# Two reorderings in a one-core audio block: ScalarE's copies of chunks 1 and 2 against a square root and a table load, and the readers of the identity against a memset

## Chip, cores and metric

The kernel runs on one core of a Trainium2 chip. The metric is the device time of one execution in microseconds (us); lower is better. A core has five engines with their own instruction streams: TensorE (PE), VectorE (DVE), ScalarE (ACT), GpSimd (POOL) and SyncE (SP, here a DMA queue). They meet only at semaphores: an instruction that has done its work increments one, and an engine waits until one has reached a value. Each engine issues in program order, so a wait holds up all that is queued behind it.

## The reference

```python
# x: (4, 32, 750); h: (4, 750, 128)
def tok(x):                       # token layer
    x_diff = first difference over time (first row 0)
    x_emb = x_diff @ W_ve.T + b_ve
    x_smooth = (ewma(x_emb) + flip(ewma(flip(x_emb)))) * 0.5     # alpha 0.1
    return x_smooth @ W_lin.T + b_lin
def attn(x):                      # 4 heads of 32
    q, k = l2norm(x @ q_w), l2norm(x @ k_w)
    v = x @ (basis @ v_coeffs.T)
    scores = (q @ k.T) * decay ** (distance - 1) * (key later than query)
    return (scores @ v) @ (basis @ o_coeffs.T).T * out_scale
def ffn(x):                       # over the 128 features
    return gelu(x @ tril(W1).T + b1) @ tril(W2).T + b2
h = tok(x)
h = h + attn(layernorm(h))
h = h + ffn(layernorm(h))
```

## The kernel before, in words

The smoothing is linear, so the kernel smooths the 32 input channels of 4 batches (128 partitions, 750 steps) to `z` and multiplies by combined weights afterwards. Time is cut into 6 chunks of 125 steps. Attention looks only forward in time, so the chunks are taken from the end: step i of the program handles chunk 5 - i, and a `state` of 32x32 per head and batch is carried on. The order on every engine is written out by hand.

**Setup.** GpSimd builds the identity (lines 263 and 265), the shifted mask `before` (267, 269), `minus_half` (271), and then writes 180.0 (`ONE`) into two rows of `z_stk` (line 274; 2 partitions x 3000 elements). It signals these with `ident_ok`, `before_ok`, `half_ok` and `zone_ok`. Behind them it waits for the feed-forward weights and cuts both to triangles (line 278), which waits for `zone_ok` too. VectorE starts with memsets: `keep` (536, 537), `keep_b` (538 to 540), `first_one`, `ones_blk` and `floor_c` (541 to 549). Then it waits for the identity and reads it twice: `centre` is the identity less 1/128 (line 551, `centre_ok`), `pick` repeats parts of it (line 552, 128x384, `pick_ok`). Behind those it works on the input: a difference (`xd`, 564), a backward scan (`bwd`, 561), a partial sum (569), two halves of the forward scan (`fwd`, 583 and 587) and `z` (575) for the last chunk, then the backward scan, difference, sum and `z` for the one before it. SyncE's queue brings the tail of `x` first, then its first half, then weights; ScalarE's queue brings the rest of `x` and `w_tok`.

**First product.** TensorE's `select` (line 838) moves `z` of a chunk into the layout of `z_stk`; it waits for `pick_ok` and `z0_ok` and stands in TensorE's order behind the product of line 825. ScalarE writes its high words (389), VectorE its low words (604), and `project_qk(0)` (917, 920) reads them, with `zone_ok` as another condition. GpSimd computes `z` of the four earlier chunks (286, 289, 292) in three passes with two inputs each; VectorE's backward scan over 500 steps (line 561) feeds the last.

**Norms.** The squared norms come in two groups: group 0 covers steps 0 and 1, group 1 steps 2 to 5. `sums` on VectorE writes them, `turn_sums` on TensorE turns them (897), `roots` on ScalarE takes the square root (456, `root_ok`), `scales` on VectorE makes the reciprocals (641, 645, 647).

**ScalarE around the change.** `roots(1)` is followed by a dummy Gelu (line 501), ahead of which the compiler puts the load of the Gelu table. Then come `q_out(2)`, `k_out(2)` (403, 410), `r_out(1)` (423) and `h_out(1)` (416), which copy PSUM banks to SBUF. TensorE's `attention_out(1)` (1026) waits for the last two. Then TensorE runs `scores(2)` (971), which waits for `root_ok`, and `ffn_turn(0)` (1047), which waits for `xn` of `normed(0)` on ScalarE (433). `normed(0)` needs `rstd` from GpSimd's `rsqrt(0)` (326, 330), which stands behind `add_b2(0)` (340) and `distance(2)` (318, needs `qT` of `q_out(2)`). The loop for steps 2 to 4 follows.

Of the kernel before, what the change touches and what calls it, by code (L numbers as in the profile page):

```python
# [7 lines left out]
ALU = mybir.AluOpType  # L8
ACT = mybir.ActivationFunctionType

B, CH, T = 4, 32, 750
D = 128
# [21 lines left out]
def build(nc, x, w_tok, w_att, w_base, w_ffn, out):  # L34
    with ExitStack() as ctx:
        def sb(name, shape, dt=F32):
            return ctx.enter_context(nc.sbuf_tensor(name, shape, dt))

        def sem(name):
            return ctx.enter_context(nc.semaphore(name))  # L40
# [3 lines left out]
        ident, centre = IC[:, 0, :], IC[:, 1, :]  # L44
        pick = sb("pick", [D, B, 3 * CH])
# [36 lines left out]
        table_in = sb("table_in", [D, 1])  # L82
# [6 lines left out]
        keep = sb("keep", [D, T])  # L89
# [17 lines left out]
        def bufs(name, shape):  # L107
# [28 lines left out]
            for n in ("s0_ps", "s1_ps", "s2_ps", "s3_ps", "r_ps", "a_ps"))  # L136
# [9 lines left out]
        pool_c, ident_ok, centre_ok, tril_ok, ones_ok, half_ok, before_ok, zone_ok, one_ok, zero_ok, floor_ok = (  # L146
            sem(n) for n in ("pool_c", "ident_ok", "centre_ok", "tril_ok", "ones_ok",
                             "half_ok", "before_ok", "zone_ok", "one_ok", "zero_ok", "floor_ok"))

        table_ok, exp_ok, dec_u, dec_ok, pow_ok, dmask_ok, keypow_ps, keypow_ok = (  # L150
            sem(n) for n in ("table_ok", "exp_ok", "dec_u", "dec_ok", "pow_ok", "dmask_ok", "keypow_ps",
                             "keypow_ok"))
# [10 lines left out]
        zstk_d, pick_ok, sel_s, selhi_ok, sello_ok = (  # L163
            sem(n) for n in ("zstk_d", "pick_ok", "sel_s", "selhi_ok", "sello_ok"))
# [18 lines left out]
        def flat(tile):  # L183
            return tile.rearrange("p b f -> p (b f)")

        def batches(part):
            return (0, B) if part is None else (part * B // 2, (part + 1) * B // 2)
# [5 lines left out]
        def turned_sums(group):  # L193
            return r_ps[0:C, 2 * D:2 * D + 2 * GR] if group == 0 else s0_ps[0:C, 0:4 * GR]
# [3 lines left out]
        def h_bank(i):  # L198
            return k1_ps if i == LAST else a_ps
# [62 lines left out]
        def _(pool):  # L262
# [8 lines left out]
            pool.memset(minus_half[:, :], -0.5).then_inc(half_ok, 1)  # L271
            pool.wait_ge(before_ok, 1)
            pool.wait_ge(half_ok, 1)
            pool.memset(z_stk[3 * CH:STK, :, :, :].bitcast(F32), ONE).then_inc(zone_ok, 1)
            pool.wait_ge(ffn_in_d, 16)
            pool.wait_ge(zone_ok, 1)
# [81 lines left out]
        def _(act):  # L358
# [39 lines left out]
            def q_out(i):  # L398
                act.wait_ge(q_s, i + 1)
                if i >= NBUF:  # L400
                    act.wait_ge(qd_ok, i - NBUF)
                    act.wait_ge(score_s, H * (i - NBUF + 1))
                act.activation(flat(qT[i % NBUF][:, :, :]), s2_ps[:, 0:W4], ACT.Copy).then_inc(qT_ok, 1)  # L403
# [8 lines left out]
            def h_out(i):  # L412
                act.wait_ge(h_s, i + 1)
                if i >= NBUF:
                    act.wait_ge(h2_ok, B * (i - NBUF + 1))
                act.activation(flat(h_tok[i % NBUF][:, :, :]), h_bank(i)[0:C, :], ACT.Copy, scale=1.0 / ONE).then_inc(h_ok, 1)  # L416

            def r_out(i, part=None):
                b0, b1 = batches(part)
                act.wait_ge(rT_s, i + 1)  # L420
                if i >= NBUF:
                    act.wait_ge(at_s, i - NBUF + 1)
                act.activation(flat(rT[i % NBUF][:, b0:b1, :]), r_ps[:, b0 * C:b1 * C], ACT.Copy).then_inc(rT_ok, 1)  # L423

            def normed(i):

                n = i % NBUF
                act.wait_ge(rstd2_ok, i + 1)
                act.wait_ge(h2_ok, B * (i + 1))
                if i >= NBUF:  # L430
                    act.wait_ge(xT_s, i - NBUF + 1)
                for b in range(B):
                    act.activation(xn[n][:, b, :], h2[n][:, b, :], ACT.Copy, scale=rstd2[n][:, b:b + 1])\  # L433
                        .then_inc(xn_ok, 1)

            def ffn_in(i, part=None):
                n, (b0, b1) = i % NBUF, batches(part)
                act.wait_ge(xT_s, done(i, part))
                if i >= NBUF:
                    act.wait_ge(f1_s, i - NBUF + 1)  # L440
                act.activation(flat(xT[n][:, b0:b1, :]), turn_bank(i, part)[:, b0 * C:b1 * C], ACT.Copy)\
                    .then_inc(xT_ok, 1)
# [9 lines left out]
            def roots(group):  # L452

                c0, c1 = GROUPS[group]
                act.wait_ge(sst_ps, group + 1)
                act.activation(nrm[:, :, c0 * B:c1 * B].rearrange("p a (c b) -> p a c b", b=B),
                               turned_sums(group).rearrange("p (c a x) -> p a c x", a=3, x=CH)[:, :, :, 0:B],
                               ACT.Sqrt).then_inc(root_ok, 1)
# [38 lines left out]
            gram_out(5)  # L497
            h_out(0)
            r_out(0)
            roots(1)  # L500
            act.activation(table_in[:, :], keep[:, 0:1], ACT.Gelu).then_inc(table_ok, 1)  # L501
            q_out(2)
            k_out(2)
            r_out(1)
            h_out(1)
            for i in range(2, LAST):
                normed(i - 2)
                ffn_in(i - 2)
                h_out(i)
                ffn_gelu(i - 2)  # L510
                q_out(i + 1)
                k_out(i + 1)
                r_out(i)
# [21 lines left out]
        def _(dve):  # L535
            dve.memset(keep[:, 0:1], 10.0 * (1.0 - ALPHA)).then_inc(keep_ok, 1)
            dve.memset(keep[:, 1:T], 1.0 - ALPHA).then_inc(keep_ok, 1)
            dve.memset(keep_b[:, 0:1], ALPHA - 1.0).then_inc(keep_ok, 1)
            dve.memset(keep_b[:, 1:2], 9.0 / ALPHA).then_inc(keep_ok, 1)
            dve.memset(keep_b[:, 2:C + 1], 1.0 - ALPHA).then_inc(keep_ok, 1)  # L540
# [4 lines left out]
            for b in range(B):  # L545
# [1 line left out]
                dve.memset(ones_blk[b * CH:(b + 1) * CH, 1, b:b + 1], 1.0).then_inc(ones_ok, 1)  # L547
            dve.memset(floor_c[0:2 * CH, :], 0.0).then_inc(floor_ok, 1)
            dve.memset(floor_c[2 * CH:GR, :], EPS_LN * ONE * ONE).then_inc(floor_ok, 1)
            dve.wait_ge(ident_ok, 1)  # L550
            dve.tensor_scalar(centre, ident, -1.0 / D, None, ALU.add).then_inc(centre_ok, 1)  # L551
            dve.tensor_copy(pick[:, :, :].rearrange("p b (a c) -> p b a c", a=3),
                            ident.rearrange("p (b c) -> p b c", b=B).unsqueeze(2).broadcast_to([D, B, 3, CH]))\
                .then_inc(pick_ok, 1)

# [78 lines left out]
            def scales(group):  # L636

                k, cols = 2 * group, slice(GROUPS[group][0] * B, GROUPS[group][1] * B)
                n = cols.stop - cols.start
                dve.wait_ge(root_ok, group + 1)  # L640
                dve.scalar_tensor_tensor(out=nrm[:, 0:2, cols], in0=nrm[:, 2:3, cols].broadcast_to([C, 2, n]),
                                         scalar=EPS_L2, in1=nrm[:, 0:2, cols], op0=ALU.mult, op1=ALU.max)\
                    .then_inc(stat_v, 1)
                dve.wait_ge(stat_v, k + 1)
                dve.reciprocal(rec[:, :, cols], nrm[:, :, cols]).then_inc(stat_v, 1)
                dve.wait_ge(stat_v, k + 2)
                dve.tensor_tensor(sc_v[:, cols], rec[:, 1, cols], rec[:, 2, cols], ALU.mult).then_inc(scale_ok, 1)
# [39 lines left out]
            def carry_on(i):  # L687

                dve.wait_ge(st_s, i + 1)
                new = flat(state[i % NBUF][:, :, :])  # L690
                if i == 0:
                    dve.tensor_copy(new, st_ps).then_inc(st_ok, 1)
                else:
                    if i >= NBUF:
                        dve.wait_ge(rT_s, i - NBUF + 2)
                    dve.wait_ge(st_ok, i)
                    dve.wait_ge(pow_ok, 1)
                    dve.scalar_tensor_tensor(out=new, in0=flat(state[(i - 1) % NBUF][:, :, :]), scalar=chunk_pow,
                                             in1=st_ps, op0=ALU.mult, op1=ALU.add).then_inc(st_ok, 1)
# [27 lines left out]
            def statistics(i, part=None):  # L727

                n, (b0, b1) = i % NBUF, batches(part)
                for b in range(b0, b1):  # L730
                    dve.wait_ge(h2_ok, B * i + b + 1)
                    dve.bn_stats(bn6[n][:, b, :], h2[n][:, b, :]).then_inc(bn_ok, 1)  # L732
                if i >= NBUF:
                    dve.wait_ge(ve2_ok, i - NBUF + 1)
                for b in range(b0, b1):
                    dve.wait_ge(bn_ok, B * i + b + 1)
                    dve.bn_aggr(mv[n][:, b, :], bn6[n][:, b, :]).then_inc(mv_ok, 1)
# [34 lines left out]
            residual(0)  # L772
            keys(1)
            statistics(0)
            scales(1)
            carry_on(1)

            for i in range(2, LAST):
                residual(i - 1)
# [411 lines left out]
```

## Time and profile before

| what | value |
|---|---|
| median of 3 runs | 84.05 us (84.0 to 87.06) |
| profiled execution, its own time | 83.98 us |
| span in its profile | 82.3 us |
| PE busy | 68.0 us (83%) |
| DVE busy | 60.6 us (74%) |
| ACT busy | 40.9 us (50%) |
| POOL busy | 37.4 us (45%) |

The span runs from the first to the last event of the engines that the profiler saw; 1.68 us of the execution's own time lie outside it. Busy times of different engines overlap. In a row of the timeline, the numbers in front are start and duration in us, "xN" the instructions merged in the row, and the bracket the idle time of that engine just before the row with the event that ended it. In the chain, each row is a piece of the sequence that ended last, with the time that it contributes.

### The profile page before, as it was taken

Reading aid. Unit: us, or ns where it says so; the run is one execution under the profiler, and the core shown is the slowest. Engines: PE = TensorE matmul, PEld = TensorE weight load, DVE = VectorE, ACT = ScalarE, POOL = GpSimd, SP = SyncE. Lnnn points to the kernel's source line nnn. Section 1 sums busy time; section 2 is a strip of 40 time slices with the busy share of each in tenths; the row PEclk is TensorE's granted clock in tenths of the full one; section 3 lists DMA queues with packets and bytes.
Section 4 is the critical chain, followed back from the end, with each engine's and each line's share of the span. In section 5 each row is a group of like instructions: output and inputs, shape, how many; then the busy total and the mean of one; then the engine's idle time right before and its main releaser. Section 6 shows DMA issues by size and latency. Waiting matters only on the chain.

```text
span 82.3 us, 2682 instructions
## 1 busy us (share of the span) xinstructions
PE 68.0 (83%) x1047; PEld 51.4 (63%) x1047; DVE 60.6 (74%) x177; ACT 40.9 (50%) x94; POOL 37.4 (45%) x48
## 2 busy tenths in 40 slices
PE   2996759964975899855999999999999997978840
PEld 2984648641143784645967996798679975845730
DVE  5799999999056493994998599848993599694250
ACT  1536345679365200494765366626663624574420
POOL 5935194396563700278423833292409100667800
PEclk9999999999999999999999999999999999999997
DMA  0960000001433100000000040003000300003043
GB/s 8 288 228 0 0 0 0 8 0 52 104 97 93 39 0 0 8 0 0 0 8 4 0 132 1 0 8 125 4 0 8 115 14 8 0 0 125 0 137 113
DMA packets 3826, 3.55 MB, mean 43 GB/s; under 512 B 2171, under 2 KB 3189, under 8 KB 3814
## 3 DMA queue, kind: packets, MB, share of 16 engines
q1 hardware_dynamic: 3474, 3.06, 12.9%
q10 hardware_dynamic: 340, 0.32, 1.2%
q8 instruction: 8, 0.13, 0.7%
q14 instruction: 4, 0.03, 0.1%
HBM read 1.08 MB, written 1.54 MB: 32 GB/s over the span
## 4 chain that ended last, share of the span: by engine, by line
PE 61%; DVE 20%; ACT 7%; issue 7%; POOL 1%; DVEq 0%; ACTq 0%; POOLq 0%
PE s_ps L971 8%; PE s_ps L1059 6%; PE a_ps L1026 6%; PE r_ps L1000 6%; PE s_ps L1076 5%; PE r_ps L986 5%; PE s_ps L875 4%; PE k_ps L929 3%; DVE prob L658 3%; PE s_ps L917 3%; DVE ident_and_centring L551 2%; PE r_ps L1047 2%; PE a_ps L951 2%; DVE ss_row L633 2%; ACT L501 2%
## 5 line engine op out<-in xcount | busy, mean ns | idle before, releaser
L658 DVE TENSOR_TENSOR prob<-s_ps,dmask 125x500 f32<-125x500 f32 x24 | 15.0, 673 | 1.7 <-PE s_ps L971 1.5
L340 POOL TENSOR_TENSOR h_b<-h,w_ffn 125x512 f32<-125x512 f32 (+1 forms) x7 | 7.8, 1133 | 11.4 <-DVE h L722 9.2
L318 POOL TENSOR_TENSOR q_dec<-qT,powers 128x500 f32<-128x500 f32 x5 | 5.8, 1163 | 9.8 <-ACT qT L403 9.8
L433 ACT ACTIVATE xn<-h,rstd 125x128 f32<-125x128 f32 x20 | 6.4, 390 | 5.8 <-POOL rstd L330 5.8
L301 POOL TENSOR_TENSOR quad<-gram_z,z 128x250 f32<-128x250 f32 (+1 forms) x6 | 5.9, 997 | 5.0 <-ACT gram_z L467 3.7
L722 DVE SCALAR_TENSOR_TENSOR h<-a_ps,rec,h_tok 125x128 f32<-125x128 f32 x22 | 6.2, 343 | 2.2 <-PE a_ps L1026 2.2
L971 PE MATMUL s_ps<-qT,kT 32*125 32x125 f32 x192 | 6.9, 279 | 0.9 <-ACT gram_z L467 0.9
L708 DVE TENSOR_TENSOR y<-s_ps,h_b 125x512 f32<-125x512 f32 (+1 forms) x6 | 3.9, 647 | 4.8 <-PE s_ps L1076 4.8
L971 PEld LDWEIGHTS s_ps<-qT,kT 32*125 32x125 f32 x192 | 5.9, 183 | 2.4 <-issue 2.1
L1026 PE MATMUL a_ps<-o_T,rT 128*125 128x128 f32 x44 | 5.9, 274 | 1.9 <-ACT h_tok L416 1.9
L330 POOL TENSOR_TENSOR rstd<-ve,minus_half 125x4 f32<-125x4 f32 (+1 forms) x7 | 6.6, 944 | 0.6
L1026 PEld LDWEIGHTS a_ps<-o_T,rT 128*125 128x125 f32 x44 | 5.3, 187 | 2.4 <-ACT rT L423 2.2
L1000 PE MATMUL r_ps<-prob,v_sc 125*32 125x125 f32 x192 | 6.4, 272 | 0.5 <-DVE prob L658 0.5
L1076 PE MATMUL s_ps<-w_ffn,gT 128*125 128x128 f32 x44 | 6.2, 283 | 0.2 <-ACT gT L449 0.2
L1000 PEld LDWEIGHTS r_ps<-prob,v_sc 125*32 125x32 f32 x192 | 4.9, 109 | 2.0 <-issue 1.8
L1059 PE MATMUL s_ps<-xT,w_T 128*128 128x500 f32 (+1 forms) x12 | 5.9, 576 | 0.0
L1076 PEld LDWEIGHTS s_ps<-w_ffn,gT 128*125 128x125 f32 x44 | 5.3, 187 | 0.9 <-issue 0.6
L986 PEld LDWEIGHTS r_ps<-q_dec,state 32*32 32x32 f32 x160 | 4.0, 104 | 2.4 <-issue 2.2
L449 ACT ACTIVATE gT<-s_ps,w_att 128x500 f32<-128x500 f32 (+1 forms) x6 | 3.9, 642 | 3.1 <-PE s_ps L1059 3.1
L986 PE MATMUL r_ps<-q_dec,state 32*32 32x125 f32 x160 | 5.3, 268 | 0.0
L423 ACT ACTIVATE rT<-r_ps 128x500 f32<-128x500 f32 (+1 forms) x7 | 3.6, 527 | 3.5 <-PE r_ps L1000 3.5
L732 DVE BATCH_NORM_STATS2 bn<-h 125x6 f32<-125x128 f32 x24 | 5.3, 278 | 0.0
(175 smaller groups left out, 147.2 us busy)
## 6 DMA issues: line engine op xcount, KB each, us to landing
out_dram<-y SPq DMA_DIRECT2D x5, 224.0 KB
z_stk<-z_hi SPq DMA_DIRECT2D x8, 62.5 KB, 2.1
z_stk<-z_lo SPq DMA_DIRECT2D x4, 62.5 KB, 2.1
out_dram<-y SPq DMA_DIRECT2D x2, 112.0 KB
w_base<-in_w_base_dram SPq DMA_DIRECT2D x1, 192.0 KB, 3.6
w_ffn<-in_w_ffn_dram SPq DMA_DIRECT2D x1, 192.0 KB, 3.6
xt<-in_x_dram SPq DMA_DIRECT2D x1, 188.0 KB, 3.0
w_tok<-in_w_tok_dram ACTq DMA_DIRECT2D x1, 162.0 KB, 3.2
```

The costliest lines, as they stand in the source:

```text
L301: pool.tensor_tensor(quad[:, a, t0:t1], gram_z[piece % 2][:, 0:t1 - t0], z[:, t0:t1], ALU.mult)\
L330: pool.tensor_tensor(rstd2[n][:, b0:b1], ve2[n][:, b0:b1], minus_half[:, b0:b1], ALU.pow)\
L340: pool.tensor_tensor(h2_b[n][:, b0:b1, :], h2[n][:, b0:b1, :], b2_row.unsqueeze(1).broadcast_to([C, b1 - b0, D]), ALU.add)\
L433: act.activation(xn[n][:, b, :], h2[n][:, b, :], ACT.Copy, scale=rstd2[n][:, b:b + 1])\
L658: dve.tensor_tensor(prob[i % 2][:, h, :, :], sc_ps[h][0:C, 0:W4].rearrange("p (b t) -> p b t", b=B), dmask[:, h, :].unsqueeze(1).broadcast ...
L722: dve.scalar_tensor_tensor(out=h2[n][:, b, :], in0=att_bank(part)[0:C, b * D:(b + 1) * D], scalar=rec[:, 0, at:at + 1], in1=h_tok[n][:, b, ...
L971: ins = pe.matmul(sc_ps[h][0:C, b * C:(b + 1) * C], kT[i % NBUF][rows, b, :], qT[i % NBUF][rows, b, :], start=True, stop=True)
L986: pe.matmul(r_ps[rows, b * C:(b + 1) * C], state[(i - 1) % NBUF][rows, b, :], q_dec[i % NBUF][rows, b, :], start=(b == 0), stop=False, ski ...
L1000: ins = pe.matmul(r_ps[cols, b * C:(b + 1) * C], v_sc[n][:, b, cols], prob[i % 2][:, h, b, :], start=(i == 0 and b == 0), stop=(b == B - 1 ...
L1026: ins = pe.matmul(att_bank(part)[0:C, b * D:(b + 1) * D], rT[n][:, b, :], o_T[:, :], start=True, stop=True)
L1059: pe.matmul(f1_bank(i, part)[:, b0 * C:b1 * C], w1_T[:, :], flat(xT[n][:, b0:b1, :]), start=True, stop=True).then_inc(f1_s, 1)
L1076: ins = pe.matmul(f2_bank(i, part)[0:C, b * D:(b + 1) * D], gT[n][:, b, :], w2_T, start=True, stop=True)
```

## The change

On VectorE, lines 550 to 554 (the wait for the identity, `centre` and `pick`) go up to stand right behind the two memsets of `keep`; all other memsets stand behind them. On GpSimd, the memset of 180.0 also waits for `centre_ok` and `pick_ok`. On ScalarE, the square root `roots(1)` and the dummy Gelu go behind the four copies. On VectorE, `carry_on(1)` goes ahead of `scales(1)`.

```diff
             pool.wait_ge(before_ok, 1)
             pool.wait_ge(half_ok, 1)
+            pool.wait_ge(centre_ok, 1)
+            pool.wait_ge(pick_ok, 1)
             pool.memset(z_stk[3 * CH:STK, :, :, :].bitcast(F32), ONE).then_inc(zone_ok, 1)
...
             r_out(0)
-            roots(1)
-            act.activation(table_in[:, :], keep[:, 0:1], ACT.Gelu).then_inc(table_ok, 1)
             q_out(2)
             k_out(2)
             r_out(1)
             h_out(1)
+            roots(1)
+            act.activation(table_in[:, :], keep[:, 0:1], ACT.Gelu).then_inc(table_ok, 1)
...
             dve.memset(keep[:, 1:T], 1.0 - ALPHA).then_inc(keep_ok, 1)
+            dve.wait_ge(ident_ok, 1)
+            dve.tensor_scalar(centre, ident, -1.0 / D, None, ALU.add).then_inc(centre_ok, 1)
+            dve.tensor_copy(pick[:, :, :].rearrange("p b (a c) -> p b a c", a=3),
+                            ident.rearrange("p (b c) -> p b c", b=B).unsqueeze(2).broadcast_to([D, B, 3, CH]))\
+                .then_inc(pick_ok, 1)
             dve.memset(keep_b[:, 0:1], ALPHA - 1.0).then_inc(keep_ok, 1)
...
             dve.memset(floor_c[2 * CH:GR, :], EPS_LN * ONE * ONE).then_inc(floor_ok, 1)
-            dve.wait_ge(ident_ok, 1)
-            dve.tensor_scalar(centre, ident, -1.0 / D, None, ALU.add).then_inc(centre_ok, 1)
-            dve.tensor_copy(pick[:, :, :].rearrange("p b (a c) -> p b a c", a=3),
-                            ident.rearrange("p (b c) -> p b c", b=B).unsqueeze(2).broadcast_to([D, B, 3, CH]))\
-                .then_inc(pick_ok, 1)
...
             statistics(0)
+            carry_on(1)
             scales(1)
-            carry_on(1)
```

## Rows read from the trace of the kernel before

**Rows 1.** Chain that ended last, whole span: start, us, what.
```profile
4.96 0.20 DVE pick L552
...
11.12 0.46 PE s_ps L917
...
34.31 1.28 ACT L501
```
**Rows 2.** Busy time by stretch, 46 to 64.3 us (PE, PEld, DVE, ACT, POOL, PEclk, DMA).
```profile
46.00:64.30 18.30, 18.30 (x336) 15.04 (x334) 14.40 (x41) 9.88 (x21) 8.45 (x9) 1.00 0.10 31
```
**Rows 3.** Timeline of VectorE, 0 to 12 us.
```profile
1.05 0.68 DVE L537 MEMSET keep<- 128x749 f32 x1
...
2.91 2.05 DVE L551 TENSOR_SCALAR ident_and_centring<-ident_and_centring 128x128 f32<-128x128 f32 x1
...
5.08 0.27 DVE L564 TENSOR_TENSOR xd<-xt 128x125 f32<-128x125 f32 x1
...
6.06 0.99 DVE L583 TENSOR_TENSOR_SCAN fwd<-keep,xt 128x375 f32<-128x375 f32 x1
...
8.28 0.29 DVE L575 TENSOR_TENSOR z<-part_z,fwd 128x125 f32<-128x125 f32 x1
...
10.28 0.74 DVE L604 TENSOR_TENSOR z_stk<-s_ps,z_stk 32x250 fp32r<-32x250 f32 x2
...
11.38 2.03 DVE L561 TENSOR_TENSOR_SCAN bwd<-keep,bwd,xt 128x500 f32<-128x500 f32 x1
```
**Rows 4.** Timeline of GpSimd, 0 to 12 us.
```profile
1.82 0.30 POOL L269 TENSOR_SCALAR_AFFINE_SELECT before<-before 125x125 f32<-125x125 f32 x1
...
2.28 2.59 POOL L274 MEMSET z_stk<- 2x3000 f32 x1
...
11.09 1.27 POOL L289 TENSOR_TENSOR part_z<-xd,fwd 128x500 f32<-128x500 f32 x1
```
**Rows 5.** Transfers of the input: KB each, median us from issue to landing.
```profile
xt<-in_x_dram SPq DMA_DIRECT2D x1, 188.0 KB, 3.0
...
xt<-in_x_dram SPq DMA_DIRECT2D x1, 63.0 KB, 2.4
```
**Rows 6.** Timeline, TensorE and then ScalarE around the first selection.
```profile
6.89 0.67 PE L825 MATMUL r_ps<-w_att,proj_T 128*98 128x256 f32 x2
...
9.39 0.80 ACT L389 ACTIVATE z_stk<-s_ps 96x250 fp32r<-96x250 f32 x2 [1.40 <-PE s_ps L838]
```
**Rows 7.** Instructions of line 278 (min/median/max ns, first and last start).
```profile
L278 POOL TENSOR_SCALAR_AFFINE_SELECT w_ffn<-w_ffn x2: 287/562/836, 6.3 to 7.1; 128x128 f32<-128x128 f32 x2
```
**Rows 8.** Timeline of ScalarE, 20 to 44 us.
```profile
34.08 0.21 ACT L456 ACTIVATE nrm<-s_ps 125x48 f32<-125x48 f32 x1 [5.25 <-PE s_ps L897]
...
37.11 0.61 ACT L416 ACTIVATE h_tok<-a_ps 125x512 f32<-125x512 f32 x1
38.88 1.28 ACT L433 ACTIVATE xn<-h,rstd 125x128 f32<-125x128 f32 x4 [1.16 <-POOL rstd L330]
```
**Rows 9.** Timeline of TensorE, 20 to 44 us.
```profile
33.97 1.07 PE L1000 MATMUL r_ps<-prob,v_sc 125*32 125x125 f32 x32
34.97 0.65 PE L951 MATMUL a_ps<-w_stk,z_stk 98*125 98x128 f32 x4
...
37.86 1.11 PE L1026 MATMUL a_ps<-o_T,rT 128*125 128x128 f32 x8 [1.85 <-ACT h_tok L416]
...
39.98 0.65 PE L1047 MATMUL r_ps<-ident_and_centring,xn 125*128 125x125 f32 x4
```
**Rows 10.** Timeline of GpSimd, 20 to 44 us.
```profile
34.49 1.28 POOL L340 TENSOR_TENSOR h_b<-h,w_ffn 125x512 f32<-125x512 f32 x1 [6.17 <-DVE h L722]
36.36 1.15 POOL L318 TENSOR_TENSOR q_dec<-qT,powers 128x500 f32<-128x500 f32 x1 [0.59 <-ACT qT L403]
...
37.80 1.05 POOL L330 TENSOR_TENSOR rstd<-ve,minus_half 125x4 f32<-125x4 f32 x1
```
**Rows 11.** Timeline of VectorE, 20 to 44 us.
```profile
36.60 0.94 DVE L647 TENSOR_TENSOR sc_v<-rec 125x16 f32<-125x16 f32 x1
```

## The prediction

> **What bounds the kernel now.** I first read the busy time by stretch, to find where TensorE is the limit. From 46 to 64.3 us it is busy for 18.30 of 18.30 us at a granted clock of 1.00 [rows 2]: a delay or a gain that arrives there is passed on to the end one for one. So the question is by how much the start of this packed stretch moves. I then followed the chain that ended last backwards. It enters the packed stretch through two places that are not TensorE's own work: VectorE's setup, with `pick` in the chain at 4.96 [rows 1], and the Gelu table load on ScalarE at 34.31 [rows 1], behind which TensorE stands still for 1.85 us until `h_tok` is copied [rows 9]. The timelines of single engines then say what these two wait for.
>
> In the setup, `centre` (line 551, 128x128) takes 2.05 us, from 2.91 to 4.96, while `pick` behind it, with three times the elements, adds 0.20 us [rows 1, 3]. Nothing about `centre` is worth 2 us. GpSimd's memset of 180.0 runs from 2.28 to 4.87 [rows 4]: `centre` is held until it ends. The same exclusion shows elsewhere. Of GpSimd's two triangle cuts the one that starts at 6.30, while VectorE's scan of line 583 runs until 7.05, takes 836 ns and the other 287 ns [rows 3, 7]; the 500-step scan of line 561 starts at 11.38, GpSimd's pass of line 289 ends at 12.36, and the scan takes 2.03 us where 375 steps took 0.99 [rows 3, 4]; and a 16-element product on VectorE (line 647) takes 0.94 us while GpSimd's line 318 runs until 37.51 [rows 10, 11].
>
> **Part 1, the setup.** The memset of `keep` ends at 1.73 [rows 3]. `centre` starts there. Its own duration isn't seen without the hold; it lies between 0.06 (a third of the 0.20 of `pick`) and 0.29 (GpSimd's free pass over this shape [rows 7]). I take 0.10, since `pick` is the same engine's work. `pick` costs 0.20. Meanwhile GpSimd has its select of `before` at 1.82, 0.30 us [rows 4], which can come between the two: 0 to 0.3 more. The other memsets filled the time from 1.73 to 2.91 [rows 3], 1.18 us, and now stand behind. The difference of line 564 so starts at 1.73 + 0.30 + 1.18 = 3.2, or 3.5 with the whole collision; I take 3.4 instead of 5.08, 1.7 us earlier. Its input (63 KB, first in SyncE's queue, issued at about 0.8) needs 2.4 us and is there at 3.2 [rows 5]. The forward scan of line 583 stood 0.98 behind line 564 [rows 3], so it starts at 4.4; its 188 KB were issued at about 1.25, need 3.0 us and land at 4.25 [rows 5]. That is just in time, and a later landing would take its part of the gain. `z` of the last chunk was finished at 8.57 [rows 3] and comes at 6.9.
>
> Not all of that arrives. TensorE's product of line 825, ahead of the selection in its order, ends at 7.56 [rows 6], and its chain (weights landed, `proj`, `proj_T`) does not move; `centre_ok` was not its last condition. The selection starts then at 7.56, not at the old 8.72 (0.67 ahead of ScalarE's 9.39). ScalarE's high words run from 7.56 + 0.67 = 8.2 to 9.0 instead of 9.39 to 10.19 [rows 6]. VectorE has finished its second `z` and the first low words of the weights by about 8.5. It takes the low words of `z_stk`, of which two instructions took 0.74 us [rows 3]: the second half cannot start before 9.05 and ends at 9.45, instead of 11.02. `project_qk(0)`, at 11.12 in the chain [rows 1], starts at 9.55: **1.6 us earlier**. VectorE and GpSimd have 0.1 us more to spare than that: GpSimd starts on the 500 steps when the second `z` is done (1.7 earlier), and so the scan of line 561, which waited for line 289 until 12.36, ends about 1.7 earlier as well. All that comes behind hangs on these engines, so I carry 1.6 us to the second place.
>
> The memset of 180.0 now starts behind `pick`, at 2.3 to 2.4 instead of 2.28, and ends by 5.0. Behind it stand the triangle cuts, which waited for their weights until 6.30 anyway [rows 7], and `project_qk(0)` needs it only at 9.55. The two added waits cost nothing unless the memset would run past 6.3; then GpSimd's three passes over `z` are late next.
>
> The point that decides part 1: the difference, sums and scans of VectorE from 3.4 on now run beside the memset. In the trace of before no instruction of VectorE with two SBUF inputs does; only its small memsets, 0.06 us each, went through beside it. The bounds of the hold are 0 and all of it, to about 4.95, where line 564 would start 0.13 earlier than before. The held rows are held by passes of GpSimd that read SBUF, or they are `centre`, and a memset reads nothing. I take 0.
>
> The Trainium skill, "SBUF — State Buffer", section "SBUF: two separate sides", says that the shared port pair is an exclusive lock for a whole instruction, taken by GpSimd or by a VectorE instruction that runs in a two-port mode, or has two SBUF inputs, the latter only against a GpSimd instruction that reads SBUF. By that rule the memset holds `centre` and `pick` but not the difference and the scans, which is the zero that I take; the trace agrees for `centre` (2.05 us), and no row shows the other half of the rule.
>
> **Part 2, the copies.** In before ScalarE waits 5.25 us, until 34.08, for the turned sums, takes the root (0.21), loads the table (1.28) and then makes four copies, the last, `h_tok`, until 37.72 [rows 1, 8]. In the new order (times still those of before) `q_out(2)` and `k_out(2)` run in the 5.25 us. `r_out(1)` waits for line 1000, which ends at 35.04, and takes until 35.65; `h_out(1)` waits for line 951, which ends at 35.62 [rows 9], and takes 0.61 [rows 8], until 36.25. `attention_out(1)` starts 0.14 later, at 36.4 instead of 37.86: 1.47 us earlier. `scores(2)` follows at 37.5 and ends at 38.6; it waits for the root, which is now taken at 36.25 and done at 36.46.
>
> Then `ffn_turn(0)` waits for `xn`, and that is late next. GpSimd's `add_b2(0)` ends at 35.77 [rows 10], unmoved, as it hangs on VectorE's residual. `distance(2)` had waited for `qT` until 36.36 and starts at 35.74: 0.62 earlier. `rsqrt(0)` follows directly, so `rstd` comes at 38.85 - 0.62 = 38.23, and ScalarE's `xn` starts at 38.26 instead of 38.88 [rows 8, 10]. The table load, now from 36.47 to 37.75, with 0.2 for the dummy, fits in front of it with 0.3 us to spare. The last `xn` is done at 39.54, and TensorE's turns end at about 40.0 instead of 40.63 (they start at 39.98 [rows 9]). **The gain that goes on is 0.6 us**, not 1.47. Bounds: 0, if VectorE's reciprocals take the port from `rsqrt(0)`, and 1.47 if `rstd` were no limit.
>
> `carry_on(1)` ahead of `scales(1)` costs nothing: the state needs TensorE's line 1012, over at 36.0, and the root comes at 36.46. But `scales(1)` has to slip between GpSimd's 318 and 330, and its last product can be held until 38.3, as it was held for 0.94 us before [rows 11]. Then the residual of step 1 starts at 38.4 instead of 39.01, still ahead of what TensorE wants of it.
>
> The Trainium skill, "ScalarE: Activation LUTs", section "What ACT_TABLE_LOAD costs", gives the load as about 1.28 us and another 1.38 us of drain. Here the load is 1.28 us and the copy behind it starts at 35.71, so no drain shows. By that page `xn` would start at 39.3, and part 2 would lose 0.4 us instead of gaining 0.6; the measured row goes.
>
> **Sum.** 83.98 - 1.6 - 0.6 = **81.8 us**. The profiled execution (83.98, span 82.3) is 0.07 below the median of 84.05, so this is 2.7% under the median. From about 2% (1.7 us) on a measurement of this kernel can tell a change from none.
>
> **Rivals.** (a) *The memset holds VectorE's two-input work too.* For it: the hold of `centre` is total, and every other overlap in the rows shows a hold. Against it: the others read SBUF. Line 564 starts at 4.95, so part 1 gives 0.1: 83.98 - 0.1 - 0.6 = 83.3. Chance 0.15.
> (b) *Part 2 gives nothing*, because VectorE's reciprocals, moved to 36.5, interleave with GpSimd's 326 and 330 and `xn` stays at 38.9. For it: line 647 and line 318 did collide. Against: the three are short (0.17 each for two of them), so that they could delay GpSimd by 0.2 to 0.3. 83.98 - 1.6 = 82.4. Chance 0.10.
> (c) *Slower: the memset of 180.0 loses the port to VectorE.* If it is not under way when VectorE's series starts at 3.4 and is shut out until the second `z` at 8.1, it ends at 10.7, the cuts (2 x 0.29) at 11.3, the first pass at 12.3, and line 289 at 13.6, holding the 500-step scan until then: it ends 1.2 later than before, and VectorE's low words of chunk 1 with it. 83.98 + 1.2 - 0.6 = 84.6; without part 2's gain 85.2. It decides from a start of the memset after about 3.4. Against: it needs only `pick`, at 2.3. Chance 0.03.
> (d) *More than forecast*: the packed work behind closes a further gap, `xn` comes sooner and part 2 brings 1.2: 81.2. Chance 0.04.
>
> **How the numbers follow.** The forecast has 0.68; its own spread (port collision 0.3, late first half of `x` 0.3, part 2 0.3 either way) is 81.4 to 82.3. The range reaches to (d) and past (a): 81.2 to 83.5. Faster by over 2% (below 82.4): the forecast, (d) and less than half of (b), 0.76. Within 2%: (a) and the rest of (b), 0.21. Slower by over 2%: 0.03, the worst of (c).
>
> **What would show it.** In the changed profile: `centre` and `pick` at 1.75 to 2.4 with no hold; the memset from about 2.4; line 564 at 3.4; line 583 at 4.4; the selection right behind line 825 at 7.6; `project_qk(0)` at 9.5; `h_tok` done 1.4 us ahead of its old place; a remaining wait of TensorE for `xn` of some 0.3 us and more ahead of line 1047. The prediction is wrong if line 564 or the scans show durations that end with the memset, or if TensorE's wait ahead of line 1047 has grown to the whole 1.47.

## The result and the profile after

The changed kernel took 82.68 us (median of 4 runs, 81.94 to 86.49) beside 84.03 us for the kernel before. The ratio of the two is 0.9765, with a 95% interval of 0.9736 to 0.9793: 2.4% less time, inside the forecast's range and with the sign that it gave. Two runs of the changed kernel, 81.94 and 82.12, are what this ratio rests on. A third took 83.23, at a granted clock of 1.00 throughout, and it is the one that was profiled (span 81.5, against 82.3 before). It is the more instructive one, since only one of the change's two parts arrives in it. The fourth run, 86.49, and all others of any kernel in which TensorE's granted clock fell to about half for 3 us or more in mid-execution are left out here and in the experiments, unless their profile is shown or the text says otherwise.

Lines of the changed kernel are numbered higher by 2 from line 274 on (the difference on 564 became 566, 825 became 827), apart from the moved ones: 551 and 552 became 541 and 542, the memsets of 538 to 549 became 545 to 556, and the dummy Gelu of 501 became 507. The timeline of VectorE in the setup:

```profile
1.65 0.16 DVE L541 TENSOR_SCALAR ident_and_centring<-ident_and_centring 128x128 f32<-128x128 f32 x1
1.72 0.35 DVE L542 COPY pick<-ident_and_centring 128x384 f32<-128x384 f32 x1
...
3.25 0.29 DVE L566 TENSOR_TENSOR xd<-xt 128x125 f32<-128x125 f32 x1
3.46 0.47 DVE L563 TENSOR_TENSOR_SCAN bwd<-keep_b,xt 128x126 f32<-128x126 f32 x1
4.04 0.29 DVE L571 SCALAR_TENSOR_TENSOR part_z<-xd,bwd 128x125 f32<-128x125 f32 x1
4.66 1.00 DVE L585 TENSOR_TENSOR_SCAN fwd<-keep,xt 128x375 f32<-128x375 f32 x1 [0.32 <-DMA xt<-in_x_dram]
...
6.86 0.37 DVE L577 TENSOR_TENSOR z<-part_z,fwd 128x125 f32<-128x125 f32 x1
...
9.46 0.43 DVE L599 TENSOR_TENSOR w_stk<-r_ps,w_stk 33x256 fp32r<-33x256 f32 x1 [1.01 <-ACT w_stk L378]
10.29 0.95 DVE L606 TENSOR_TENSOR z_stk<-s_ps,z_stk 32x250 fp32r<-32x250 f32 x2 [0.40 <-ACT z_stk L391]
```

VectorE has what it was to have: `centre` in 0.16 us instead of 2.05 [rows 3], the difference at 3.25 instead of 5.08, `z` at 6.86 instead of 8.28. But then it waits, 1.01 and 0.40 us, for ScalarE, which waits for TensorE. The timeline of TensorE says why:

```profile
4.85 0.74 PE L815 MATMUL a_ps<-w_tok 128*128 128x98 f32 x2 [0.35 <-DMA w_tok<-in_w_tok_dram]
...
7.52 0.64 PE L824 MATMUL k_ps<-w_base 128*128 128x128 f32 x2
7.95 1.06 PE L827 MATMUL r_ps<-w_att,proj_T 128*98 128x256 f32 x2
8.80 1.59 PE L840 MATMUL s_ps<-z,pick 128*96 128x125 f32 x8
...
11.34 0.47 PE L919 MATMUL s_ps<-z_stk,w_stk 98*128 98x500 f32 x1 [0.53 <-DVE z_stk L606]
```

The pair of line 827 takes 1.06 us instead of 0.67 and starts at 7.95 instead of 6.89 [rows 6]; the selection, which nothing holds any more, takes 1.59. `project_qk(0)` starts at 11.34, later than the 11.12 of before [rows 1]. The second place, the copies of chunks 1 and 2, moved as forecast. ScalarE first, then GpSimd and TensorE:

```profile
35.64 0.60 ACT L418 ACTIVATE h_tok<-a_ps 125x512 f32<-125x512 f32 x1
36.13 0.20 ACT L458 ACTIVATE nrm<-s_ps 125x48 f32<-125x48 f32 x1
36.35 1.28 ACT L507 ACT_TABLE_LOAD   x1
37.65 0.20 ACT L507 ACTIVATE table_in<-keep 128x1 f32<-128x1 f32 x1
38.23 1.28 ACT L435 ACTIVATE xn<-h,rstd 125x128 f32<-125x128 f32 x4 [0.37 <-POOL rstd L332]
```
```profile
35.70 1.16 POOL L320 TENSOR_TENSOR q_dec<-qT,powers 128x500 f32<-128x500 f32 x1
36.83 0.23 POOL L328 TENSOR_SCALAR ve<-mv 125x4 f32<-125x4 f32 x1
37.15 1.04 POOL L332 TENSOR_TENSOR rstd<-ve,minus_half 125x4 f32<-125x4 f32 x1
```
```profile
36.38 1.11 PE L1028 MATMUL a_ps<-o_T,rT 128*125 128x128 f32 x8 [0.39 <-ACT h_tok L418]
37.42 1.15 PE L973 MATMUL s_ps<-qT,kT 32*125 32x125 f32 x32
38.77 1.11 PE L1049 MATMUL r_ps<-ident_and_centring,xn 125*128 125x125 f32 x4 [0.20 <-ACT xn L435]
39.64 0.72 PE L931 MATMUL k_ps<-w_stk,z_stk 98*125 98x256 f32 x4
```

`attention_out(1)` starts at 36.38 instead of 37.86, `xn` at 38.23 instead of 38.88 [rows 8, 9]. The turns (line 1049) take 1.11 instead of 0.65 us, because TensorE now waits between them for each `xn`, and the product behind them starts at 39.64 instead of 40.39, by the same timeline of before. That is 0.75 us, and the spans differ by 0.8: this execution had part 2 and nothing of part 1.

### The profile page after: what moved, and what is told of

It is laid out like the page before. It is cut to its first block, busy times and chain, and to the rows that moved or that the text cites. A ratio compares the mean times of both kernels' runs of the same rounds, so it can differ in the third digit from the quotient of the medians.

```text
span 81.5 us, 2683 instructions
## 1 busy us (share of the span) xinstructions
PE 70.0 (86%) x1047; PEld 53.1 (65%) x1047; DVE 58.4 (72%) x177; ACT 41.1 (50%) x94; POOL 37.1 (45%) x48
## 2 busy tenths in 40 slices
DMA packets 3826, 3.55 MB, mean 44 GB/s; under 512 B 2171, under 2 KB 3189, under 8 KB 3814
## 4 chain that ended last, share of the span: by engine, by line
PE 65%; DVE 9%; issue 9%; POOL 4%; DMA 4%; ACT 4%; ACTq 1%; DVEq 0%; POOLq 0%
PE s_ps L973 7%; PE s_ps L1061 6%; PE r_ps L1002 6%; PE s_ps L1078 5%; PE r_ps L988 5%; PE a_ps L1028 5%; DMA w_tok<-in_w_tok_dram 4%; PE s_ps L877 4%; PE k_ps L931 4%; DVE prob L660 3%; DVE h L724 3%; PE r_ps L1049 3%; PE s_ps L919 3%; PE a_ps L953 2%; PE s_ps L840 2%
## 5 line engine op out<-in xcount | busy, mean ns | idle before, releaser
L405 ACT ACTIVATE qT<-s_ps 128x500 f32<-128x500 f32 x6 | 3.5, 586 | 7.0 <-PE s_ps L919 7.0
```

## The experiments

Beside e1 to e8 the kernel before took 83.96 to 84.08 us (from e5 to e8 in only two runs of seven). Beside e9 to e12 it took 85.43 us or more in all seven runs, at a mean granted clock of 0.96 to 0.98, and a ratio to these would credit the experiments with the clock. So from e5 on the times themselves are compared, with 83.96 to 84.08 and with those of e4 and e11.

**One part alone.** e1 is the changed kernel with part 2 undone, e2 the kernel before with part 2 alone.

```diff
@@ e1: back on ScalarE, and likewise scales(1) ahead of carry_on(1) on VectorE
+            roots(1)
+            act.activation(table_in[:, :], keep[:, 0:1], ACT.Gelu).then_inc(table_ok, 1)
             q_out(2)
...
-            roots(1)
-            act.activation(table_in[:, :], keep[:, 0:1], ACT.Gelu).then_inc(table_ok, 1)
```

> The changed kernel with part 2 undone: roots(1) and the dummy Gelu back ahead of the four copies, scales(1) back ahead of carry_on(1); only VectorE's reordering of centre and pick and GpSimd's two waits are left. If part 1 is worth the 1.6 us that the prediction gives it, the time is 82.4 us. If TensorE's matmuls ahead of the first selection run at the half pace that they show in the profile after (0.63 against 0.42 us for line 827's), part 1 gives nothing and the time is 83.9 to 84.2 in that execution. If TensorE's place behind line 825 takes more than predicted, something between.

Its lowest run took 82.47 us, which is the forecast for part 1. The other three (84.05, 84.16, 85.81) all had a fall of the granted clock. The profiled one, 84.16, has `project_qk(0)` at 9.86, 1.26 us earlier than before, still has `attention_out(1)` 1.25 us earlier (36.61), and lost this gain again from about 37.6 on, when the granted clock fell. The view by stretch, and TensorE's `scores(2)`, which takes 1.15 us elsewhere:

```profile
34.00:37.00 3.00, 1.15 (x39) 1.00 (x39) 2.48 (x11) 2.45 (x6) 2.33 (x4) 1.00 0.00 0
37.00:41.00 4.00, 4.00 (x46) 3.66 (x45) 2.34 (x7) 1.51 (x5) 1.85 (x2) 0.58 0.00 0
```
```profile
37.65 2.06 PE L973 MATMUL s_ps<-qT,kT 32*125 32x125 f32 x32
```

So e1 shows that part 1 can bring 1.5 to 1.6 us, in one run. It doesn't say how often, or what decides.

> The kernel before with part 2 alone: the four copies ahead of roots(1) and the Gelu table, carry_on(1) ahead of scales(1). By the prediction 0.6 us, 83.4. The profile after shows TensorE's kv product of step 2 at 39.64 with the first part unmoved, against 40.5 before, so 0.75 us would make 83.25. The rival that part 2 gives nothing expects 84.0.

It took 83.28, 83.24, 83.31 and 83.22, a ratio of 0.991 (0.9893 to 0.9927). Part 2 is worth 0.8 us, and each time. The rival of no gain is out. (In the profile before, `attention_out(1)` is at 37.86 and `xn` at 38.88; here they are at 36.40 and 38.26, as in the profile after.)

**What decides part 1.** e3 is the changed kernel again, e4 has one more warm-up product.

> The changed kernel once more. The theory: the executions split by TensorE's pace in the setup. Where w_tok lands before the warm-up products of line 811 end (about 4.5 us), the products of lines 817 to 827 take the short durations of the profile before, project_qk(0) starts at about 9.6 to 9.8 and the time is near 82.0; where it lands later, TensorE is idle for 0.3 us, the durations stay long, project_qk(0) starts at 11.3 and the time is near 83.2. Rival: the split comes from something later, and the short executions show the same setup as the profile after.

All four runs took 83.11 to 83.61 (ratio 0.9922, 0.9889 to 0.9955). The profile of one of them:

```profile
5.11 0.75 PE L815 MATMUL a_ps<-w_tok 128*128 128x98 f32 x2 [0.61 <-DMA w_tok<-in_w_tok_dram]
...
8.21 1.06 PE L827 MATMUL r_ps<-w_att,proj_T 128*98 128x256 f32 x2
9.06 1.36 PE L840 MATMUL s_ps<-z,pick 128*96 128x125 f32 x8
...
11.38 0.46 PE L919 MATMUL s_ps<-z_stk,w_stk 98*128 98x500 f32 x1 [0.53 <-DVE z_stk L606]
```

There was no short execution here to look at, so of the two halves of the theory only the slow one is seen: `w_tok` late, TensorE idle for 0.61 us, long products, `project_qk(0)` at 11.38. The highest of the four, 83.61, had a mean granted clock of 0.979, so it can belong to either kind of setup. Of the six other runs of this kernel that count, two took about 82.0 and four 83.1 to 83.5.

```diff
-WARM = 6
+WARM = 7
```

> The changed kernel with 7 instead of 6 warm-up products that nobody reads, 0.49 us more, so that TensorE has no idle time until w_tok is there at 4.4 to 4.8. If the idle time ahead of line 815 decides TensorE's pace, every execution is short: median at 82.1 to 82.5 (the extra product itself can put line 815 up to 0.4 us later), and none at 83.2 or more. If the pace is decided by something else, the spread of the changed kernel stays (81.9 to 83.2) and 0 to 0.4 us come on top.

All four runs took 81.55 to 81.85, 0.9722 of before (0.9701 to 0.9742), and better than the changed kernel's best. In the profile the idle time is gone and the products become short on the way:

```profile
4.72 0.59 PE L815 MATMUL a_ps<-w_tok 128*128 128x98 f32 x2
...
5.87 0.38 PE L818 MATMUL k_ps<-ident_and_centring,w_tok 128*98 128x128 f32 x2
...
6.88 0.67 PE L827 MATMUL r_ps<-w_att,proj_T 128*98 128x256 f32 x2
7.39 1.02 PE L840 MATMUL s_ps<-z,pick 128*96 128x125 f32 x8
...
9.41 0.46 PE L919 MATMUL s_ps<-z_stk,w_stk 98*128 98x500 f32 x1 [0.58 <-DVE z_stk L606]
```

One warm-up product of 0.43 us takes about 1.6 us off the more frequent kind of execution (median 81.66 against 83.1 to 83.5).

> The kernel before with a seventh warm-up product and nothing else. Theory: TensorE's pace in the setup costs the kernel before nothing, since its first selection waits for VectorE's z until 8.7 whatever the pace; so the time stays at 83.9 to 84.1, though the products of lines 815 to 825 may be shorter. Rival: the seventh product helps any version, by the 1.5 us that it brought to the changed kernel: 82.5.

It took 83.96 us in the one run that counts, the same as before, so the seventh product shows no gain of its own. Its profile (of the run of 85.57, whose clock fell behind the setup) has a second point: there is no idle time ahead of line 813, and the products are still long until 7.2 (line 821's pair in 0.65 us, line 822's in 0.40). It costs nothing, since the selection waits for `z` until 8.72:

```profile
7.50 0.59 PE L825 MATMUL r_ps<-w_att,proj_T 128*98 128x256 f32 x2
8.72 1.06 PE L838 MATMUL s_ps<-z,pick 128*96 128x125 f32 x8 [0.63 <-DVE z L575]
```

The other way to close the gap is to let `w_tok` land earlier (e6, 6 warm-up products):

```diff
-            act.dma_start(xt[:, MID:TAIL], x[:, MID:TAIL]).then_inc(x_mid, 16)
             act.dma_start(WT[:, :], w_tok).then_inc(tok_in, 16)
+            act.dma_start(xt[:, MID:TAIL], x[:, MID:TAIL]).then_inc(x_mid, 16)
```

> The changed kernel with 6 warm-up products, and on ScalarE's queue the transfer of w_tok ahead of that of the middle of x, so that w_tok lands some 0.4 us earlier and TensorE goes from its warm-up into line 815 with no idle time. If the idle time is what keeps the products slow, the median is 81.5 to 82.1 and none of its executions is near 83.2. If it takes the extra warm-up work itself, the executions stay at 82 to 83.4.

The runs took 81.67 to 81.80. In the profile (of the run of 84.70, whose clock fell later), line 815 starts at 4.29 without a wait, line 827's pair at 6.94 in 0.67 us, `project_qk(0)` at 9.55. It is the absence of the gap, not the extra product, that goes with the short products. And none of the fourteen runs that count of the versions without a gap (e4, e6, and e7, e8 and e11 below) took more than 82.1.

**Which half of part 1 does the work.** Both on the kernel of e4. e7 leaves out GpSimd's two waits:

```diff
-            pool.wait_ge(centre_ok, 1)
-            pool.wait_ge(pick_ok, 1)
```

> The changed kernel with 7 warm-up products and without GpSimd's two waits. The memset of 180.0 can start at 2.3 as in the profile before, and centre and pick on VectorE are done at 2.1, ahead of it. Theory: VectorE's move alone does the work, time as with the waits, 81.6 to 81.7. Rival: centre or pick is caught by GpSimd's earlier instructions and the memset, and VectorE loses up to 2.6 us: 83.3.

The runs took 81.69 to 82.07. In the setup of the profiled one (86.99, its clock fell later) the memset starts at 2.39 and `xd` at 3.25, as with the waits. They are not needed for the time. e8 keeps them and puts `centre` and `pick` back behind the memsets of VectorE:

> The changed kernel with 7 warm-up products and GpSimd's two waits, but centre and pick on VectorE back behind all memsets. They then run from 2.91 to 3.3 with nothing held, and the difference of line 564 starts at 3.3, as in the changed kernel; the memset of 180.0 runs from 3.3 to 5.9, still ahead of the 6.2 at which the triangle cuts start. Theory: the wait alone does the work as well, 81.6 to 81.8. Rival: the later memset holds something on VectorE or comes late for its readers, 82.5 or more.

The one run that counts took 81.69. In the profile (of a run of 83.14) `centre` and `pick` run unheld from 2.91, the difference starts at 3.32 and `project_qk(0)` at 9.53:

```profile
2.91 0.23 DVE L553 TENSOR_SCALAR ident_and_centring<-ident_and_centring 128x128 f32<-128x128 f32 x1
3.05 0.35 DVE L554 COPY pick<-ident_and_centring 128x384 f32<-128x384 f32 x1
3.32 0.28 DVE L566 TENSOR_TENSOR xd<-xt 128x125 f32<-128x125 f32 x1
```

Either half alone takes the hold of 2 us away. The later memset on GpSimd (3.55 to 6.14) is over ahead of the triangle cuts, which waited for their weights until 6.74.

**Does a reading GpSimd instruction hold VectorE's two-input work?** e10, again on the kernel of e4, puts eight selects in front of the memset of 180.0 (they write a tile `spare` that nobody reads; its lines stand 5 higher from here on):

```diff
+            for n in range(8):
+                pool.affine_select(out=spare[:, n, :], in_=ident, compare_op=ALU.not_equal, fill=1.0, base=0,
+                                   pattern=[[-1, D]], channel_multiplier=1).then_inc(pool_c, 1)
+            pool.wait_ge(pool_c, 10)
             pool.memset(z_stk[3 * CH:STK, :, :, :].bitcast(F32), ONE).then_inc(zone_ok, 1)
```

> The changed kernel with 7 warm-up products and, ahead of GpSimd's memset of 180.0 and behind its two waits, eight selects of 128x128 that read the identity and write a spare tile that nobody reads, 0.29 us each, from 2.4 to about 4.7. VectorE's difference (line 566 in the changed kernel, from 3.25) and its scans now run beside GpSimd instructions that read SBUF, where in the changed kernel a memset ran that reads nothing and they kept 0.29 and 0.47 us. If only a reading GpSimd instruction holds VectorE's two-input work, these instructions lengthen by up to 0.3 us each, or GpSimd's selects do, and selects and memset end later. If nothing of the kind holds them, the durations stay. The time itself: 81.65 to 82.5.

It took 81.68, 82.08 and 82.08, against 81.70 to 81.88 in e11, and the effect is small. VectorE:

```profile
3.25 0.39 DVE L571 TENSOR_TENSOR xd<-xt 128x125 f32<-128x125 f32 x1
3.56 0.50 DVE L568 TENSOR_TENSOR_SCAN bwd<-keep_b,xt 128x126 f32<-128x126 f32 x1
4.17 0.36 DVE L576 SCALAR_TENSOR_TENSOR part_z<-xd,bwd 128x125 f32<-128x125 f32 x1
```

and the selects, by their tile:

```profile
L278 POOL TENSOR_SCALAR_AFFINE_SELECT spare<-ident_and_centring x8: 288/292/401, 2.5 to 4.3; 128x128 f32<-128x128 f32 x8
```

The difference is longer by 0.10, the scan by 0.03, the sum by 0.07; one of the eight selects is longer by 0.11. Beside a scan of 0.50 us the selects ran on at 0.29. The sign is that of the expectation, the size is at its low end, and a lock held for the whole of either instruction would show more.

The other direction stands in the profiles too, and there the hold is long. The triangle cuts are selects as well, and the first of them starts beside a scan over 375 steps:

```profile
5.76 1.00 DVE L589 TENSOR_TENSOR_SCAN fwd<-keep,fwd,xt 128x375 f32<-128x375 f32 x1
```
```profile
6.17 0.93 POOL L280 TENSOR_SCALAR_AFFINE_SELECT w_ffn<-w_ffn 128x128 f32<-128x128 f32 x2 [1.20 <-DMA w_ffn<-in_w_ffn_dram]
```

These are of the profile after: the first cut takes 677 ns, the second 288. In six profiles (before, after, e1, e2, e3, e5) the first cut starts 0.40 to 0.75 us ahead of the end of such a scan, takes 491 to 836 ns, and ends 0.09 us behind the scan each time. So a scan that was under way held a select that came later until its end, while selects that were under way in e10 cost a scan of 126 steps 0.03 us. The runs don't say what makes the difference, and don't separate the theories cleanly.

**VectorE's order and the limit of part 2**, both on the kernel of e4. e11 puts `scales(1)` ahead of `carry_on(1)` again.

> The changed kernel with 7 warm-up products and VectorE's order undone: scales(1) ahead of carry_on(1). carry_on(1) then waits for the root at about 34.7 and comes some 1.3 us later, but project_kv(2) wants the state only at 37.97, so the theory expects no change, 81.6 to 81.7. Rival: the order mattered, 82 or more.

The runs took 81.70, 81.75 and 81.88: no change, as worked out. e9 moves `add_b2(0)` on GpSimd behind `rsqrt(0)`:

```diff
-                add_b2(i - 1)
+                if i > 1:
+                    add_b2(i - 1)
                 distance(i + 1)
                 rsqrt(i - 1)
+                if i == 1:
+                    add_b2(i - 1)
```

> The changed kernel with 7 warm-up products, and GpSimd's add_b2(0) moved from ahead of distance(2) to behind rsqrt(0). Theory: what limits part 2 to about 0.75 us of the 1.47 by which h_tok is earlier is GpSimd, whose distance(2) stood behind add_b2(0). Counted from the profile of the run with 7 warm-up products: distance(2) can run at about 31.5, in ScalarE's former wait, rsqrt(0) starts when VectorE's statistics are done at about 34.4 instead of 35.15, rstd is there at 35.7; then the Gelu table and its dummy, until 36.1, are the last ahead of xn, instead of 36.55. TensorE's turns come 0.45 us earlier: 81.2. Rival: something else holds TensorE ahead of the turns (scores end at 36.85 there), 81.65 as without the move.

It took 81.02, 81.04, 81.37 and 81.96 (the last two at mean granted clocks of 0.991 and 0.994, the first two at 1.00), against 81.70 to 81.88 in e11. Its lines stand 3 higher behind the moved call. GpSimd:

```profile
32.13 1.16 POOL L320 TENSOR_TENSOR q_dec<-qT,powers 128x500 f32<-128x500 f32 x1 [5.25 <-ACT qT L408]
34.71 0.23 POOL L328 TENSOR_SCALAR ve<-mv 125x4 f32<-125x4 f32 x1 [1.41 <-DVE mv L742]
35.02 1.05 POOL L332 TENSOR_TENSOR rstd<-ve,minus_half 125x4 f32<-125x4 f32 x1
```

and ScalarE and TensorE:

```profile
36.22 0.20 ACT L510 ACTIVATE table_in<-keep 128x1 f32<-128x1 f32 x1
36.33 1.26 ACT L438 ACTIVATE xn<-h,rstd 125x128 f32<-125x128 f32 x4
```
```profile
34.95 1.11 PE L1031 MATMUL a_ps<-o_T,rT 128*125 128x128 f32 x8 [0.39 <-ACT h_tok L421]
...
37.07 0.90 PE L1052 MATMUL r_ps<-ident_and_centring,xn 125*128 125x125 f32 x4
37.73 0.72 PE L934 MATMUL k_ps<-w_stk,z_stk 98*125 98x256 f32 x4
```

From the start of `attention_out(1)` to the product behind the turns it is now 2.78 us (37.73 - 34.95), against 3.27 in e4 (37.97 - 34.70) and 3.26 in the profile after: 0.49 us less, where 0.45 was expected. `xn` starts directly behind the dummy Gelu, so the table load is the next limit, and GpSimd was the one before.

> The changed kernel with 6 warm-up products, w_tok first on ScalarE's queue, and add_b2(0) behind rsqrt(0). If both effects are what they were taken for and add up, 81.79 less 0.45 gives 81.3.

The runs took 81.16, 81.28 and 81.31, as expected. The two versions e9 and e12 beat both kernels: 81.02 and 81.16 at best, 3.0 and 2.9 us under the 84.03 of before. The 84.03 were not taken beside them, but e11 was, and they are 0.5 us under it.

## Why the prediction was right, and where it was not

**The hold of `centre`: right.** 2.05 us became 0.16, where 0.10 was taken; GpSimd's select beside it grew from 0.30 to 0.41, where 0 to 0.3 was allowed; the difference of line 564 came at 3.25 (3.4 forecast).

**The zero for the memset beside the two-input work: right.** In the profile after, the memset runs from 2.38 to 4.97, and beside it the difference takes 0.29 and the scan 0.47 us (before, alone: 0.27 and 0.47). Rival (a) is out, and (c) too: the memset started at 2.38. This is the half of the rule of the Trainium skill, "SBUF — State Buffer", section "SBUF: two separate sides", that no row of before showed, and this case's trace agrees with it. The reason given for the zero, that the other holds are by passes that read SBUF, is supported only in part: by e10, selects that read SBUF cost VectorE 0.03 to 0.10 us each time, not their whole length. The strong holds of the rows of before are those by GpSimd's two-input passes [rows 3, 4, 10, 11], that of an instruction with one input by the memset, and that of the first triangle cut by VectorE's scan, which came again in five more profiles.

**The first half of `x`: mis-sized.** It landed 3.4 us after its issue in the profile after and 3.6 in e3 (3.0 forecast), and line 585 waited 0.32 and 0.55 us for it. The prediction had said that a later landing takes its part. In e4, where it landed on time, line 585 started at 4.31 and `z` was done at 6.83, ahead of the end of line 827 (7.55).

**TensorE's place ahead of the selection: the step that failed.** The prediction took the end of line 825, 7.56, for fixed, since its chain of conditions does not move. The conditions don't, but the pace does. With the same six warm-up products and the same order of transfers, the pair of this line ended at 7.56 (before), 8.05 (e1), 8.30 (e2), 9.01 (after) and 9.27 (e3), and the profile before was the quick one. The sum was right in form: with TensorE quick, `project_qk(0)` came at 9.41 to 9.62 (e4, e6, e7, e8, e10, e11), where 9.55 was forecast, and part 1 brought about 1.6 us (e4 against e2). Where the short products began later, it came at 9.66, 9.86 and 10.10 (e9, e1, e12). With TensorE slow it came at 11.34 and 11.38, and part 1 brought nothing. The kernel before could not show this: its selection waited for `z` until 8.72, which covers a line 825 that ends at 8.3 (e2: its pair starts at 7.63, 0.42 us of waiting are left and `project_qk(0)` is at 11.12 as ever). Part 1 took exactly this cover away. I take this for the reason that the times of before lie within 0.12 us (and those of e2, with the same setup, within 0.09), and those of the changed kernel in two groups, near 82.0 and near 83.3. No profile of the first group exists, so its quick setup is inferred from e4 and e6. The forecast of 81.8 is that of the first group and misses it by 0.1 to 0.3; for the other group, four runs of six, it was too good by 1.3 to 1.7 us. That the ratio on record came out as forecast is luck in part: it rests on the two runs of the first group, and e3, whose runs were all slower, measured 0.9922, which is 0.7 us.

**Part 2: right, a little small.** `attention_out(1)` at 36.38 (36.4 forecast), `xn` at 38.23 (38.26), and GpSimd as the next limit, which e9 shows. 0.6 us were forecast and 0.75 to 0.8 measured. The term that was mis-sized is the end of the turns: they ended at 39.88 (38.77 + 1.11), where 40.0 was forecast, only 0.37 behind the last `xn` (38.23 + 1.28). The root behind the copies, `carry_on(1)` and `scales(1)` cost nothing, as said (e11), though the hold fell elsewhere than forecast: the first product of `scales(1)` took 0.54 us, until GpSimd's line 320 was over at 36.86, and the last its free 0.17. GpSimd's 328 and 332 kept their durations (0.23, 1.04), so rival (b) is out by mechanism too. The drain of 1.38 us of the Trainium skill, "ScalarE: Activation LUTs", section "What ACT_TABLE_LOAD costs", does not show here either: the dummy Gelu starts 0.02 us after the load's end.

**What is still open.** What the chip's decision on TensorE's pace hangs on exactly. In the two profiles with 0.35 and 0.61 us of idle time ahead of line 815, the products stayed long until about 10; in e1 and e2, with 0.14 and 0.04 us, until 6.8 and 7.6; without any, until between 4.7 and 7.8. So without a gap the short products began by 7.8 in every profile, but the moment wanders by some 3 us for reasons that these profiles don't show (e5 and e12 have no gap, and it comes at 7.2 and about 7.7). An artificial gap of a chosen length was not tried. Nor do the runs say whether the late landing of `w_tok` (3.6 and 3.8 us after the issue in the two profiles with the wide gap, 3.1 to 3.5 in the others with the same order of transfers) is chance or has to do with the change.

## What to carry to other kernels

Before a wait is shortened, ask what else it was covering: here the wait of the selection for `z` hid a TensorE that runs at half its pace in some executions, and with the wait gone the gain came only when TensorE was quick. A setup that is read from one profile should be checked for durations that differ between equal instructions (421 against 275 ns for the same product), and the warm-up should reach past the latest landing of the first operand, not the usual one. Where a long memset on GpSimd stands beside a short one-input instruction on VectorE, put either of them elsewhere; one of the two is enough.

## What the runs showed of the hardware

- A GpSimd memset that reads nothing held a one-input tensor instruction of VectorE for 2 us, but neither memsets of VectorE nor its scans and sums with two SBUF inputs (0.29 and 0.47 us beside it).
- TensorE's pace in the setup does not show in the granted clock of the profile. Between 4.80 and 10.20 in the profile after it reads 1.00, while the pair of line 827 takes 634 ns each instead of 379 and 458:

```profile
4.80:10.20 5.40, 5.35 (x24) 5.07 (x25) 3.80 (x8) 2.46 (x9) 2.56 (x5) 1.00 0.11 40
```
```profile
L827 PE MATMUL r_ps<-w_att,proj_T x2: 634/634/634, 7.9 to 8.4; 128*98 128x256 f32 x2
```

  The falls later in an execution do show there (0.58 from 37 to 41 us in e1). The Trainium skill, "TensorE: Matmul & The Clock Gate", section "Part 1: The HAM clock gate (the "warmup" mystery)", describes a default of half the rate that activity releases. The durations agree with that, though the row above reads 1.00, so that the level is inferred from the durations alone: I take the long ones for those of the lower of its two levels (1.2 GHz) and the short ones for those of the higher (2.4 GHz), 421 and 275 ns for one product of line 824, 286 and 162 ns for one weight load of line 827 (profile after and e4).
- A scan of VectorE over 375 steps (two SBUF inputs) held a GpSimd select that came later until 0.09 us behind its own end, in six profiles (491 to 836 ns instead of 288). Selects already under way lengthened a difference, a scan and a sum of VectorE by 0.10, 0.03 and 0.07 us only (e10).
- The landing of one and the same 162 KB transfer varied from 3.1 to 3.8 us after its issue, with the same transfers around it.
